# A pause between the value product and its transposes in the key/query/value generator of an attention layer on eight cores

## The reference

```
xn = layernorm(x)                                  # 4096 x 1024
kqv = xn @ W_kqv.T                                 # keys, queries, values
score = q @ k.T / sqrt(1024) + slope[h] * (n - s)  # ALiBi bias, slope = 2 ** (-(h + 1) / 2)
s = softmax(score) @ v
g = silu(ffn(xn))                                  # three cycles of out + coupling(out) * twist(out)
x = x + s * g
```

## Time and profile before

| what | value |
|---|---|
| time, median of 3 runs | 2886.17 us (2881.59 to 2976.6) |
| profiled execution, its own time | 2886.17 us |
| span of the profiled execution, slowest core (core 6) | 2884.6 us |
| spans of the other cores | 2861.0 to 2880.3 us |
| mean granted TensorE clock of core 6 (1 is full speed) | 0.881 |
| attention stage on core 6, first projection to last value product | 207.4 to 1723.7 us |

### The profile page before, as it was taken

The page is one execution under the profiler, slowest core; times in us unless marked ns, Lnnn a source line. Parts: engine busy times, 40 slices in busy tenths (PEclk is TensorE's granted clock), DMA queues, the critical chain, the costliest instruction groups (busy, mean ns, idle before and its releaser), DMA issues.

```text
span 2884.6 us, 32583 instructions; the slowest of 8 cores (2861.0 to 2884.6 us)
## 1 busy us (share of the span) xinstructions
PE 2193.7 (76%) x8756; PEld 905.5 (31%) x8756; DVE 826.8 (29%) x1315; ACT 1464.9 (51%) x2366; POOL 100.9 (3%) x150
## 2 busy tenths in 40 slices
PE   0245888888898899888888884688888888863665
PEld 0232323232232223322222223433333333322544
DVE  1566322121011000110000004533443544545333
ACT  0221454757876898779999980033333333323000
POOL 1000000000000000000000000000000000002332
PEclk9667899899999899999999995699999999985555
DMA  9610210000000000000000005544444444424655
GB/s 181 164 30 8 52 30 10 21 8 15 8 8 8 9 8 1 8 8 8 8 9 8 8 8 150 151 105 102 110 99 109 106 102 107 101 67 127 204 193 179
DMA packets 343974, 190.21 MB, mean 66 GB/s; under 512 B 303419, under 2 KB 321981, under 8 KB 343694
## 3 DMA queue, kind: packets, MB, share of 16 engines
q1 hardware_dynamic: 323470, 160.08, 21.2%
q0 software_dynamic: 3696, 11.27, 2.8%
q10 hardware_dynamic: 16640, 16.78, 2.0%
HBM read 165.30 MB, written 36.96 MB: 70 GB/s over the span
## 4 chain that ended last, share of the span: by engine, by line
PE 46%; DVE 15%; ACT 15%; issue 11%; DMA 5%; DVEq 4%; POOL 1%; ACTq 1%; SPq 0%; another core or an unknown queue 0%; POOLq 0%
ACT PBUF L465 14%; PE PA L703 12%; PE PC L457 4%; PE PA L457 4%; PE PA L374 3%; PE PC L374 3%; PE PD L439 3%; DMA XT<-x 3%; PE PBp L439 3%; PE PD L441 2%; DVE STATE L819 2%; DVE TMP L810 2%; DVE SBF L788 2%; DVEq L822 2%; DVEq L816 2%
## 5 line engine op out<-in xcount | busy, mean ns | idle before, releaser
L465 ACT ACTIVATE PBUF<-PC,ebias_s 128x512 bf16<-128x512 f32 x972 | 667.8, 793 | 212.4 <-PE PC L457 117.7
L465 ACT ACTIVATE PBUF<-PA,ebias_s 128x512 bf16<-128x512 f32 x972 | 667.5, 789 | 165.4 <-PE PC L457 107.4
L457 PE MATMUL PC<-QT,KT 64*128 64x512 bf16 x972 | 350.8, 391 | 74.3 <-ACT PBUF L465 54.5
L703 PE MATMUL PA<-SBF,W1S 128*128 128x512 bf16 x1536 | 357.5, 396 | 25.4 <-DVE SBF L788 21.7
L457 PE MATMUL PA<-QT,KT 64*128 64x512 bf16 x972 | 323.7, 393 | 40.5 <-ACT PBUF L465 22.0
L714 ACT ACTIVATE H<-PA,b1c_s 128x512 bf16<-128x512 f32 x192 | 131.9, 687 | 345.7 <-PE PA L703 345.7
L485 DVE COPY SRW<-PBp 65x1024 f32<-65x1024 f32 x32 | 39.1, 1220 | 745.5 <-PE PD L441 745.5
L439 PE MATMUL PD<-PBUF,VB 128*65 128x512 bf16 x528 | 211.3, 400 | 30.2 <-ACT PBUF L465 16.7
L810 DVE TENSOR_TENSOR TMP<-PD,STATE 128x512 f32<-128x512 f32 x192 | 123.6, 686 | 362.2 <-PE PD L802 356.8
L703 PEld LDWEIGHTS PA<-SBF,W1S 128*128 128x128 bf16 x1536 | 154.1, 101 | 228.9 <-issue 66.5
L441 PE MATMUL PD<-PBUF,VB 128*65 128x512 bf16 x528 | 210.0, 398 | 0.0
(11 more groups left out here) (109 smaller groups left out, 1847.9 us busy)
## 6 DMA issues: line engine op xcount, KB each, us to landing
W1S<-w1b_s SPq DMA_DIRECT2D x192, 256.0 KB, 2.9
W2S<-w2b_s SPq DMA_DIRECT2D x96, 256.0 KB, 2.9
XTs<-x SPq DMA_DIRECT2D x8, 2048.0 KB, 31.5
sraw_s<-SRW SPq DMA_DIRECT2D x64, 256.0 KB
XT2s<-x SPq DMA_DIRECT2D x16, 1024.0 KB, 5.6
XT<-x SPq DMA_DIRECT2D x32, 512.0 KB, 4.1
SINB<-sraw_s ACTq DMA_DIRECT2D x16, 1024.0 KB, 5.8
out<-OUT SPq DMA_DIRECT2D x32, 512.0 KB, 2.9
```

The lines of the kernel that those rows point to most:

```text
L457: inst = TE.matmul(RING[r], lhs, QT[b][hh * 64:(hh + 1) * 64, sc * SC2:(sc + 1) * SC2], start=True, stop=True)
L465: inst = SE.activation(out=PB_[slot][:], in_=RING[r], func=AF.Exp, bias=ebias[:, h * 32 + nt: h * 32 + nt + 1], scale=1.0 / 32.0)
L703: inst = TE.matmul(HALF[slot][:], W1S[wslot][:, ft * 128:(ft + 1) * 128], sbf[:, ft * TC:(ft + 1) * TC], start=(ft == 0), stop=(ft == NF - 1))
```

## The change

In a value step the generator now yields once more, between the copy to `VSTG` and the transposes. What was one step becomes two. The token of the copy is kept in a variable, so that the later wait is for this copy and not for what may have been counted since.

```diff
                     inst = VE.tensor_copy(out=VSTG[j][:], in_=RING[r])
                     vKV.inc(inst)
                     ring_tok[r] = (vKV, vKV.n)
+                    cp_tok = vKV.n
+                    yield
                     r2 = ring_next()
-                    TE.wait_ge(vKV.h, vKV.n)
+                    TE.wait_ge(vKV.h, cp_tok)
                     for k in range(4):
                         inst = TE.transpose(RING[r2][:, k * 128:(k + 1) * 128],
                                             VSTG[j][:, k * 128:(k + 1) * 128], identf[:])
```

## The result

The changed kernel takes 2834.02 us (median of 8 runs, 2825.76 to 2838.55); the kernel before, beside it, 2884.13 us. The ratio is 0.983, with a 95% interval of 0.981 to 0.985: 1.7% less, clearly faster and still inside 2%. The forecast was 2851 us, 35 us less.

What follows compares the result with a forecast made beforehand. No engine bounds throughout; ScalarE paces attention, but value steps sit wholly on the path. Savings of 18.7 + 8.9 + 5.0 + 1.0 + 1.5 = 35.1 us took 2886.2 to 2851.1 us, range 2834 to 2870.

Steps and rivals of the forecast that it cites:

- The wait for the copy goes in 30 of 36 steps: Value steps: a unit covers the copy, so TensorE idle before the transposes falls from 35.2 to about 6 us.
- The projection half costs what a key step costs: Value step's first half: eight matmuls and a copy, priced like a key step at 1.51 us over plain units.
- pair 3: Attention stage: 5 separated value steps, one unit apart, saving 1.00 us each, 5.0 us in all.
- The transposes cost 0.45 to 0.56 us: Transposes as own step: 0.45 us where two or three units lie between steps, 0.56 where only one does.
- pairs 5 and 6: Attention stage: 16 value steps, all separated, saving 1.17 us each, 18.7 us in all.
- pair 4: Attention stage: 8 value steps saving 1.11 us each, 8.9 us in all.
- The clock was left at what it was: TensorE's granted clock: no term in the sum, only a few microseconds of range for drops of 1.58 us each.
- The 1.5 us that the forecast gave to steps at the end of a query group: Value steps meeting the SRW copies on VectorE: the score no longer waits, 0.6 us in two or three places.
- entirely hidden: Rival, attention stage: the transposes cost nothing, each separated step saves 1.62 us, 48.6 in all, 2837.6 us; chance 0.11.
- A wait that moved: Rival: VectorE finishes the copy late, the 0.98 us stall reappears before transposes or fourth score, 2886 us; chance 0.04.
- transposes that wait for an exponential: Rival: the transposes' ring half is still in use, ScalarE idles 2.42 us, 2910.2 us; both slower rivals together 0.03.
- a clock drop at each transposition: Rival: each separate transposes step costs a 1.58 us clock drop, 2898.5 us; both slower rivals together 0.03.

Runs made afterwards that it cites:

- y1: Kernel before, with a second VectorE copy of VSTG onto itself that the transposes wait for: 2903.48 us against 2882.26, ratio 1.008.
- y2: Changed kernel, with a second VectorE copy of VSTG onto itself that the transposes wait for: 2836.28 us, ratio 0.984 to the kernel before.
- x1: Kernel before, with a second, empty yield behind each value step, projection and transposes left together: 2878.03 us against 2886.06, ratio 0.996.

## Why the prediction was right, and where its size was off

- *The wait for the copy goes in 30 of 36 steps.* Right: 5.7 us of idle time are left of 35.2 (forecast 6), and y1 and y2 show that the wait was paid one for one before and is covered now.
- *The projection half costs what a key step costs.* Right: 1.50 against 1.51 where two or three units follow. Where one unit follows, as in pair 3, both cost more: the key step that starts at 617.83 us in the kernel before has one unit and 4.02 us up to the next step, 1.71 over plain. The forecast used 1.51 there too, so pair 3 saved 0.86 us a step and not 1.00.
- *The transposes cost 0.45 to 0.56 us.* This is the first term that was mis-sized: in pairs 5 and 6 they cost 0.27. The argument from the earlier trace rows was at fault. There, after many plain units, the first score comes 0.54 us ahead of its exponential, just in time. Two or three units after an insertion TensorE is further ahead, because ScalarE is still working off a queue. The trace of the kernel before shows that in the third unit behind a value step (the transposes of the changed kernel stand one unit further on):

```profile
905.59 0.60 PE L457 MATMUL PC<-QT,KT 64*128 64x512 bf16 x2
...
906.40 1.28 ACT L465 ACTIVATE PBUF<-PC,ebias_s 128x512 bf16<-128x512 f32 x2
```

  The score starts 0.81 us ahead of its exponential, so it has 0.27 us to spare, and 0.56 us of transposes would cost 0.29. The forecast did not look at these rows. Against it the periods give 0.19 us more in 16 steps, 0.23 more in the 8 of pair 4 (where the forecast counted on one unit between the parts, and half of the time there are two) and 0.14 less in the 5 of pair 3: together 4.2 us.
- *The clock was left at what it was.* The second, and the larger: the forecast gave it only a few microseconds of the range, and it was worth some 8.7. In these runs the time at the lower level went the way of the waits (130.7 us with the longer wait of y1, 108.5 before, 79.6, 80.2 and 76.2 where the waits are gone), but x1 moved it too with no wait removed. What sets it is not shown.
- Of the 48.9 us by which the stage fell in the mean of the cores, 37.8 follow from the periods, some 8.7 from the clock, and about 2 in pair 3 come from the spacing of the steps by something else than the clock (x1). The 1.5 us that the forecast gave to steps at the end of a query group were not measured by themselves; no more than a microsecond is left for them, less than the means can tell.
- *The range.* It held, by luck: 2834.02 us against a lower end of 2834, with three of the eight runs at 2825.76 to 2830.44. The range had taken the clock as drops that come or go one by one, and the clock gave more than that. The rival "entirely hidden" (2837.6) is close in time but not what happened: the transposes do cost something, and the clock made up the rest. A wait that moved, transposes that wait for an exponential, and a clock drop at each transposition did not occur: the stretch of both parts ran at a clock of 1.00. The rule that short idles between groups of matmuls make the clock swing (the Trainium skill, TensorE: Matmul & The Clock Gate, "A second HAM failure mode: psum-queue depth-cycling") is borne out in part: the single value period of the kernel before ran at 1.00 with its idle of 0.94 us, but over the stage the clock rose from 0.95 to 0.96 as these idles went, though the groups of matmuls became more and shorter.

## What to carry to other kernels

In this kernel, and presumably wherever one engine sets the pace and another feeds it through a few buffers, what is put between two feeds costs its length less what the feeding engine is ahead by. Here that was about 0.3 us where two or more units stood between two insertions, and about 0.1 where only one did (a projection with 1.82 us to the next score cost 1.50 and 1.71). So split what is put in, above all at a point where it would wait for a third engine, and let the feeding go on in between; price the parts by an insertion of the same kind that already stands in the trace, not by the quiet stretches. A step that waits for the result of its own first half can also take up the previous step's second half: it removed the wait just as well here, and also where steps stand in a row, though a step costs more that way (2.15 us against 1.77). And a change of TensorE's stalls can be worth more than their length, as in y1 (15 us of added copying, a stage 25 us longer): compare the granted clock over the whole stage, not only in the periods.

## What the runs showed of the hardware that was not expected

The granted clock reacted to where the work stands, with all waits in place: over pair 3 it was 0.93 to 0.96 on the eight cores before, and 0.95 to 1.00 when only an empty step had been added to the generator (x1); the 406 matmuls were busy for 101.04 us at 0.93 and for 95.92 us at 1.00. A microsecond at the lower level cost the stage about 0.3 us (0.32 and 0.30 from core to core in two executions). Eight f32 transposes in a row start 0.107 us apart, so that four more cost 0.43 us.
